# 64x64 score products of 192 keys, two copies on another engine, a fourth place for probabilities

## What is computed

```python
def local_attention(q, k, v):          # 8 heads of 64, WINDOW = 128
    bk, bv = (look_around(bk), look_around(bv))     # own window and the one before it
    sim = jnp.einsum('bhwid,bhwjd->bhwij', bq, bk)
    mask = (i < j) | (i > j + WINDOW) | (j == -1)
    sim = jnp.where(mask, -jnp.finfo(sim.dtype).max, sim)
    attn = jax.nn.softmax(sim, axis=-1)
    out = jnp.einsum('bhwij,bhwjd->bhwid', attn, bv)
...
h = h @ w1 + b1
a, g = jnp.split(h, 2, axis=-1)
h = a * jax.nn.gelu(g, approximate=False)
x = x + h @ w2 + b2                    # hidden width 682
```

## Time and profile before

| | |
|---|---|
| time, median of 3 runs (lowest, highest) | 1422.82 us (1421.16, 1426.13) |
| the profiled execution: its time, its span | 1424.29 us, 1422.5 us |
| granted TensorE clock over the span | 0.991 of full |
| busy: PE, PEld, DVE, ACT, POOL | 97%, 74%, 68%, 62%, 54% |

### The profile page before, as it was taken

The page is one execution under the profiler, slowest core; times in us unless marked ns, Lnnn a source line. Parts: engine busy times, 40 slices in busy tenths (PEclk is TensorE's granted clock), DMA queues, the critical chain, the costliest instruction groups (busy, mean ns, idle before and its releaser), DMA issues.

```text
span 1422.5 us, 24115 instructions
## 1 busy us (share of the span) xinstructions
PE 1374.8 (97%) x7740; PEld 1050.5 (74%) x7740; DVE 963.8 (68%) x2671; ACT 878.1 (62%) x2223; POOL 762.1 (54%) x522
## 2 busy tenths in 40 slices
PE   6999997999999999999999999999999999999988
PEld 5878775777777777777777777786777777777756
DVE  6877765767676666666667777676767676766657
ACT  4556656575747575747475766666565757575763
POOL 2425765564647373738373747464655646473710
PEclk9999999999999999999999999999999999999998
DMA  7111100000000000000001010000000000000046
GB/s 220 38 51 60 55 30 1 1 1 0 0 0 0 0 0 0 0 0 0 0 1 60 14 47 1 1 0 0 0 0 0 0 0 0 0 0 0 0 145 210
DMA packets 35243, 33.33 MB, mean 23 GB/s; under 512 B 8364, under 2 KB 32896, under 8 KB 35200
## 3 DMA queue, kind: packets, MB, share of 16 engines
q1 hardware_dynamic: 35200, 32.79, 7.3%
HBM read 24.39 MB, written 8.39 MB: 23 GB/s over the span
## 4 chain that ended last, share of the span: by engine, by line
PE 78%; ACT 11%; DVE 5%; issue 4%; POOL 1%; DMA 0%; ACTq 0%; SPq 0%; DVEq 0%; POOLq 0%
PE l_psF L1399 9%; PE l_psP L842 9%; PE l_ring L842 9%; PE l_ring L1399 8%; PE l_ring L1469 7%; ACT l_att L1073 7%; PE l_psP L1453 6%; PE l_psF L1487 6%; PE l_psS L1410 5%; PE l_psS L1422 4%; PE l_ring L653 3%; PE l_psF L1439 2%; PE l_psS L671 1%; PE l_psP L688 1%; ACT L1163 1%
## 5 line engine op out<-in xcount | busy, mean ns | idle before, releaser
L955 POOL TENSOR_TENSOR l_att<-l_att 128x1024 f32<-128x1024 f32 x64 | 153.1, 2403 | 315.7 <-DVE l_att L880 315.7
L1007 POOL TENSOR_TENSOR l_att<-l_att,l_rinv 128x1024 f32<-128x1024 f32 x64 | 126.4, 1975 | 70.7 <-DVE l_rinv L1243 70.4
L1053 ACT ACTIVATE l_att<-l_psP 128x384 f32<-128x384 f32 (+1 forms) x128 | 70.3, 549 | 120.7 <-PE l_psP L1453 120.4
L1248 DVE COPY l_att<-l_psP 128x384 f32<-128x384 f32 (+1 forms) x128 | 78.9, 617 | 86.7 <-PE l_psP L1453 82.5
L1453 PE MATMUL l_psP<-ident,l_att 128*128 128x128 f32 x896 | 124.5, 279 | 2.0 <-DVE l_att L1248 1.5
L1453 PEld LDWEIGHTS l_psP<-ident,l_att 128*128 128x128 f32 x896 | 98.6, 141 | 32.4 <-issue 28.2
L962 POOL TENSOR_TENSOR l_att<-l_att,l_rn 128x1024 f32<-128x1024 f32 x64 | 120.8, 1910 | 0.7 <-ACT l_rn L861 0.5
L1073 ACT ACTIVATE l_att<-l_psF,l_nb 128x256 f32<-128x256 f32 x256 | 118.1, 483 | 2.1 <-DVE l_nb L1236 2.1
L971 POOL TENSOR_TENSOR l_u_lo<-l_att,l_u_hi 128x512 fp32r<-128x512 f32 x75 | 95.7, 1288 | 39.1 <-ACT l_u_hi L1048 39.0
L1469 PE MATMUL l_ring<-l_att 128*64 128x256 f32 (+1 forms) x1024 | 112.5, 362 | 2.0 <-ACT l_att L1053 1.4
L1236 DVE CUSTOM_DVE_ANT_0 l_psF<-l_psF,w_mask 128x256 f32<-128x256 f32 x256 | 101.1, 456 | 16.3 <-issue 16.3
(11 more groups left out here) (209 smaller groups left out, 4037.2 us busy)
## 6 DMA issues: line engine op xcount, KB each, us to landing
a_tables<-in_x SPq DMA_DIRECT2D x8, 512.0 KB, 4.3
scratch_s<-a_o SPq DMA_DIRECT2D x8, 512.0 KB, 3.2
l_att<-in_x SPq DMA_DIRECT2D x8, 512.0 KB, 8.8
l_att<-scratch_s SPq DMA_DIRECT2D x8, 512.0 KB, 9.0
out_dram<-l_att SPq DMA_DIRECT2D x7, 512.0 KB, 7.8
aw_stage<-in_wqkv SPq DMA_DIRECT2D x2, 768.0 KB, 5.9
l_att<-in_wqkv SPq DMA_DIRECT2D x2, 768.0 KB, 5.4
w_w_raw<-in_w SPq DMA_DIRECT2D x2, 640.0 KB
```

What stands on the lines that cost most here:

```text
L955: pool.tensor_tensor(rot[:, t, :], rot[:, t, :], t2[t % 2], ALU.add).then_inc(S["added"], 1)
L1007: pool.tensor_tensor(pr, pr, along(inv, 2 * P), ALU.mult).then_inc(S["p_done"], 1)
```

## The change

Score products are cut in two along the queries. Each is then 64 queries by the 192 keys that these can see (64 queries by 128 keys in the first window), and the four products of a window (two halves, two heads) fall on the four 64x64 quarters of the array. Key columns that are no longer computed hold what was there; the mask covers them as before. In steps with a feed-forward part, the first window of unit 1 keeps its 128-query form. The waits of a unit's scores stand in a function of their own, `score_operands`, which is called before the last product of the group that goes ahead of them. Hidden tile 5 of `down` goes behind the transposes of unit 1. In the 14 like steps ("wide") there are four places for probabilities, the fourth in a part of `ffn_buf`, and the exponentials of unit 5 stand before the ScalarE copy of unit 2's transposes. `u_high` of tiles 4 and 5 goes from ScalarE to VectorE, as the maximum of the tile with itself.

```diff
+HACT = HT - 2
+BAND = P // 2
...
-    Pr = (probs[:, 0, :], probs[:, 1, :], rot[:, 2, :])
+    Pr = (probs[:, 0, :], probs[:, 1, :], rot[:, 2, :], ffn_buf[:, 0:2, :].rearrange("p a b -> p (a b)"))
+    def place_of(u, wide):
+        return u % (4 if wide else 3)
...
-        def softmax(i, u, ffn):
-            ge(act, S["pT_ps"], UNITS * i + u - 2)
+        def softmax(i, u, ffn, wide):
+            place = place_of(u, wide)
+            ge(act, S["pT_ps"], UNITS * i + u - (3 if wide else 2))
...
-                if ffn and j:
+                if ffn and 0 < j <= HACT:
                     u_high(i, j - 1, attn)
...
-                    if 3 <= u < UNITS + 3:
+                    if 3 <= u < UNITS + 3 and not (wide and u == 5):
                         p_evac(i, u - 3)
                     if u < UNITS and (ffn or u):
-                        softmax(i, u, ffn)
-                    if u == 1 and ffn:
-                        u_high(i, HT - 1, attn)
+                        softmax(i, u, ffn, wide)
+                    if wide and u == 5:
+                        p_evac(i, u - 3)
...
+        def u_high(i, j, attn):
+            rows = P if j < HFULL else HREM
+            ge(dve, S["u_done"], HT * (i - 1) + j + 1)
+            u = gate_of(j, attn)[0:rows, :]
+            dve.tensor_tensor(U_hi[0:rows, j, :], u, u, ALU.max).then_inc(high_done(i, j)[0], 1)
...
                 if ffn:
                     gated(i, j, lf, attn)
+                if attn and ffn and j == HACT:
+                    u_high(i, j, attn)
...
-                        least_of(i, u)
+                        least_of(i, u, wide)
+                    if u == 1 and ffn:
+                        u_high(i, HT - 1, attn)
                     if 1 <= u <= UNITS:
-                        inverse_sum(i, u - 1)
+                        inverse_sum(i, u - 1, wide)
...
-        def scores(i, u, tiles=0):
+        def score_operands(i, u, tiles=TT):
+            if u < 2:
+                ge(pe, S["qT_sb"], TT * i + tiles)
+                ge(pe, S["kT_sb"], TT * i + tiles)
+            else:
+                ge(pe, S["exp_done"], UNITS * i + u - 1)
+        def scores(i, u, whole=0):
             pair, half = u // 2, u % 2
...
-                c0 = 0 if t else P
                 for par in range(2):
                     rows = slice(par * DH, (par + 1) * DH)
-                    last = pe.matmul(ps[:, par * 512 + tt * 2 * P + c0:par * 512 + (tt + 1) * 2 * P], QT[rows, pair, t * P:(t + 1) * P],
-                                     KT[rows, pair, max(t - 1, 0) * P:(t + 1) * P], start=True, stop=True, skip_group_check=True)
+                    c = par * 512 + tt * 2 * P - (t - 1) * P
+                    for part in range(1 if tt < whole else 2):
+                        n = P if tt < whole else BAND
+                        q = t * P + part * BAND
+                        k0, k1 = (q - P, q + n) if t else (0, P)
+                        last = pe.matmul(ps[part * BAND:part * BAND + n, c + k0:c + k1], QT[rows, pair, q:q + n], KT[rows, pair, k0:k1],
+                                         start=True, stop=True, skip_group_check=True)
...
                 ge(pe, S["u_done"], HT * (i - 1) + HFULL)
+                scores(i, 1, 1)
...
-                down(i, 0, range(0, 4))
+                down(i, 0, range(0, 4), ahead=2 if attn else None)
...
-                    if ffn and u in (2, 4):
-                        down(i, 0, range(3 + u // 2, 4 + u // 2))
+                    if ffn and u == 2:
+                        down(i, 0, range(4, 5), ahead=3)
...
-                        p_transposes(i, u - 3)
+                        p_transposes(i, u - 3, wide, u + 1 if ffn and u + 1 < UNITS and u != 4 else None)
+                    if ffn and u == 4:
+                        down(i, 0, range(5, HT), ahead=5)
```

More of the change, by code:

```diff
@@ L1079, in step @@
             turn = attn and ffn and la != lf
+            wide = attn and ffn and not turn
             def square():
@@ L1402, in hidden, with down @@
                 last.then_inc(S["w1_ps"], 1)
-        def down(i, c, tiles):
+        def down(i, c, tiles, ahead=None):
             for k in tiles:
@@ L1450, in p_transposes @@
                     for own in (range(2) if u % 2 or tt else (1,)):
+                        if ahead is not None and par and tt and own:
+                            score_operands(i, ahead)
                         src = par * 512 + tt * 2 * P + own * P
                         dst = par * 512 + (tt * 2 + own - (0 if u % 2 else 1)) * P
-                        last = pe.transpose(psP[:, dst:dst + P], Pr[u % 3][:, src:src + P], ident[:, :])
+                        last = pe.transpose(psP[:, dst:dst + P], Pr[place_of(u, wide)][:, src:src + P], ident[:, :])
             last.then_inc(S["pT_ps"], 1)
```

65 lines of the change are left out of this document (36 added, 29 removed).

## The result

| | before | after |
|---|---|---|
| time, median of 10 runs (lowest, highest) | 1422.67 us (1421.05, 1426.13) | 1427.35 us (1425.55, 1428.82) |
| ratio, 95% interval | | 1.0027 (1.0019, 1.0035) |
| span of the profiled execution, granted clock | 1422.5 us, 0.991 | 1426.6 us, 0.991 |

What follows compares the result with a forecast made beforehand. TensorE nearly fills the kernel (78% of the chain). Shorter score products and the stall removed at unit 7, less new holds, give 0.65 us a step: 14 x 0.65 = 9.1, forecast 1413.7 us, range 1404 to 1427.

Steps and rivals of the forecast that it cites:

- waits ahead: Waits put ahead of the last product before a unit's scores: save nothing, a fulfilled wait being unseen in the rows.
- the stall of 0.66: TensorE ahead of unit 1's transposes: new 0.66 us wait for VectorE's copy of unit 0, formerly covered by tile 5's `down`.
- The score products: TensorE, four quarters at once: odd unit 0.81 us (0.26 less), even 0.70 (0.155 less), units 0 and 1 0.05 more.
- The first rival: Score products run only two quarters at a time: group 0.32 us, 2.4 us a step slower, 1457 us; chance 0.13.
- the overlap in part: Rival for the score products: one slot more in each unit, 0 to 0.25 us a step gained, 1421 us; chance 0.18.
- the 1.2 us: TensorE's own work in the score products, summed over the units: 1.2 us a step less.
- My walk: Trace times moved through one like step: unit 0's exponentials about 0.4 us earlier, final lead 0.65 us a step.
- The copy of tile 4: `u_high` moved to VectorE: falls into idle 0.65 us ahead of 1186.39, costs nothing; otherwise minima about 0.6 later.
- the last transpose of unit 0: TensorE: last of six transposes waits for unit 2's exponentials, held 0.43 us, leaving 0.1 of 0.4 gained.
- The rival that had them save time (1406): Early waits save the 0.1 us entry of each group: 1.1 to 1.25 us a step gained, 1406 us; chance 0.11.
- The stall at unit 7: TensorE idle 0.53 us ahead of unit 7's scores, counted as 0.6 a step; gone once unit 5's exponentials end earlier.
- given back at the transposes of unit 3: TensorE: ScalarE's copy of unit 2 runs later, so these transposes start at 1201.23 us, before 1201.05.

Runs made afterwards that it cites:

- g2: Kernel before with only the four places and unit 5's exponentials ahead of ScalarE's copy of unit 2; 1417.0 us, ratio 0.9964.
- h3: Kernel before with the four places, unit 5's exponentials first, and the waits of units 2 to 7 ahead of the last product; 1425.3 us, ratio 1.0018.
- h5: Changed kernel with both copies on ScalarE and `down` of tile 5 in its old place; 1420.1 us, ratio 0.9984.
- e1: Changed kernel with the copy of tile 4 back on ScalarE, all else as changed; 1420.6 us, ratio 0.9983.
- e3: Kernel before with quarters for the score products and the waits ahead; copies, places and order as before; 1428.0 us, ratio 1.0030.
- f3: Kernel before, old score products, with only the waits of units 2 to 7 ahead of the last product; 1432.3 us, ratio 1.0065.
- e4: Changed kernel with `down` of tile 5 back ahead of the transposes of unit 1; 1426.5 us, ratio 1.0020.
- g1: Changed kernel with tile 4's copy made from PSUM and `down` of tile 5 back in its old place; 1420.1 us, ratio 0.9980.

## Why the prediction was wrong

Forecast was 0.65 us a step less; it became 0.19 more. Along the chain of runs from before to after, the periods give each part:

| part | forecast | measured |
|---|---|---|
| four places, unit 5's exponentials first (g2) | about -0.4 (0.6 gained, 0.18 given back) | -0.40 |
| waits ahead (h3 beside g2) | 0 | +0.39 |
| quarters (h5 beside h3) | the rest of the gain | -0.16 |
| copy 5, `down` 5 moved (e1 beside h5) | 0 and the stall of 0.66 | -0.06 |
| copy 4 on VectorE (after beside e1) | 0 | +0.42 |

The second and third row rest on the trace of h3; by medians they are about +0.58 and -0.37.

- **The score products.** Right in TensorE's own time: 0.81 for an odd unit, 0.70 for an even one (forecast the same), units 0 and 1 1.83 together (forecast 1.77). The first rival, two quarters at a time, is refuted: 16 records in 0.81 us; so is the overlap in part, with one slot more a unit. What failed is how much of the 1.2 us comes through: 0.34 without the places (e3 beside f3), 0.16 to 0.37 with them, since ScalarE sets the start of unit 3's transposes and VectorE that of the values behind unit 7. My walk had the exponentials of unit 0 earlier by 0.4; they came 0.4 later.
- **The copy of tile 4: the step that failed.** "On VectorE it falls into an idle 0.65 ahead of 1186.39 and costs nothing there; without that cover it would push the minima back by about 0.6." The idle time was there, but the instruction took 1.60, since GpSimd was reading. The prediction has a price of about 0.6 for it, from no row of VectorE, and does not look at what GpSimd did then. The 0.9 by which the minima came late is worth 0.42 a step, and 1.5 more around step 8, which I had put at nothing.
- **The waits ahead: the second step that failed.** "The waits put ahead of the last product save nothing by this count" is right, but the walk has a hold in one place, the last transpose of unit 0. There are three. In e1, where the copy does no harm, the last products of tiles 3 and 4 are held too (1186.57 and 1188.40 below), the scores behind them start at 0.43 in place of 0.32, and even the hold of 0.04 at 1186.57 costs the whole 0.11. The rival that had them save time (1406) had the wrong sign.

```profile
1186.30 0.40 PE L1438 MATMUL l_ring<-l_u_lo,w_w_hi 128*128 128x512 f32 x1
1186.57 0.50 PE L1438 MATMUL l_ring<-l_u_hi,w_w_lo 128*128 128x512 f32 x1
1187.00 0.78 PE L1475 MATMUL l_psS<-l_att 64*64 64x128 f32 x16
...
1188.04 0.40 PE L1438 MATMUL l_ring<-l_u_lo,w_w_hi 128*128 128x512 f32 x1
1188.40 0.50 PE L1438 MATMUL l_ring<-l_u_hi,w_w_lo 128*128 128x512 f32 x1
1188.83 0.88 PE L1475 MATMUL l_psF<-l_att 64*64 64x192 f32 x16
```

- **The new stall at the transposes of unit 1**: forecast 0.66, measured 0.69. Right in size, and nearly without worth (0.05 and 0.02 in e4 and g1), because the transposes of unit 3 wait behind ScalarE in any case.
- **The stall at unit 7** is gone; given back at the transposes of unit 3 were to be 0.18, and in g2 it is 0.2.

So 0.42 + 0.39 of the 0.84 missed are the two steps; they are differences of runs in one order of edits, and in another order they come out otherwise (the waits ahead cost 0.65 on the kernel before, the copy 0.36), and the 0.39 is the less certain of the two, as said under h3. The residue is not assigned. What quarters with a wait at the scores themselves would bring stays open.

## What to carry to other kernels

Before you move an instruction into another engine's idle time, list what GpSimd runs in that window, and price an f32 copy or maximum of VectorE from SBUF to SBUF by the end of GpSimd's instruction if they meet; here an operand from PSUM avoided it. A wait moved ahead of a product was free here only where it was long fulfilled: leave it where a change of shape already stops the engine. And make each part of a compound change alone: here one part was worth -0.40 and two others some +0.4 each. Where one trace is to carry a difference of 0.2 a step, hold it against the medians as well.

## What the runs showed of the hardware

- A VectorE copy of 128x512 f32 from SBUF to SBUF beside GpSimd's: 1.60 us with two inputs, 1.33 with one. Of 42x512 with GpSimd idle: 0.68 and 0.41. GpSimd, which came first, kept its 1.27. Where VectorE's two-input instruction (0.65) came 0.17 ahead of GpSimd's, GpSimd's took 2.24 in place of 1.89.
- A product of 512 columns held for 0.04 us (the shortest hold that was seen) to 0.44 costs about 0.11 more until the next group, and shows as 0.50 in place of 0.40, mostly without a mark of idle time. For a held transpose it is 0.05 to 0.06 (0.25 to 0.26 to the scores in place of 0.20). A product of two columns between groups of different shape costs 0.12.
- Records of f32 products on the four 64x64 quarters start four within 0.02 us, and the next four 0.16 later (192 columns; 0.20 behind the first four of a group); on halves of 64x128 before, two at a time and the next two 0.21 later (256 columns; 0.31 behind the first two). Each group's 16 and 8 records stand one after the other in the program.
